# Attention block on one core: the tail's norms scaled on ScalarE, its row products and sums on GpSimd, the outputs' high half a step later

## What is computed

```python
x  = x + ga * attention(layernorm(x) * (1 + ca) + sa)      # x1 in the kernel
h  = layernorm(x) * (1 + cb) + sb                          # first norm of the tail
x  = x + gb * (layernorm(h) * ln_g + ln_b)                 # second norm of the tail
```

## Time and profile before

| | |
|---|---|
| median of 3 runs | 3386.67 us (3384.64 to 3388.11) |
| the profiled execution | 3387.18 us, span 3385.4 us |
| TensorE products busy | 3043.3 us (90%) |
| VectorE busy | 2615.7 us (77%) |
| ScalarE busy | 1756.1 us (52%) |
| GpSimd busy | 1780.8 us (53%) |
| chain that ended last | PE 43%, DVE 22%, issue 12%, POOL 6%, ACT 6% |

### The profile page before, as it was taken

How to read it: one execution, slowest core, us unless ns; L and a number is a source line. 1 busy time by engine, 2 the same in 40 slices (tenths; PEclk the granted TensorE clock), 3 DMA queues, 4 the chain that set the end, 5 groups by cost and what they waited for, 6 DMA issues and landing times.

```text
span 3385.4 us, 59145 instructions
## 1 busy us (share of the span) xinstructions
PE 3043.3 (90%) x21664; PEld 1165.7 (34%) x21664; DVE 2615.7 (77%) x4326; ACT 1756.1 (52%) x3411; POOL 1780.8 (53%) x1617
## 2 busy tenths in 40 slices
PE   3799999889989999989998999999898999999895
PEld 1323333424343332424333243433424333242221
DVE  4687777897768788797877878788786878878577
ACT  3416565655655554665545555565544555555551
POOL 2404444473536656473664736566473655736454
PEclk8769999999999999999999999999999999999997
DMA  5302020312031120312103031221313112021122
GB/s 207 101 12 63 16 69 14 95 41 71 17 95 44 43 69 31 97 45 77 45 28 111 29 92 32 62 63 29 98 32 107 32 45 80 26 76 44 40 80 69
DMA packets 180875, 205.27 MB, mean 61 GB/s; under 512 B 21460, under 2 KB 137428, under 8 KB 179428
## 3 DMA queue, kind: packets, MB, share of 16 engines
q1 hardware_dynamic: 180584, 201.50, 20.6%
HBM read 114.09 MB, written 36.50 MB: 44 GB/s over the span
## 4 chain that ended last, share of the span: by engine, by line
PE 43%; DVE 22%; issue 12%; POOL 6%; ACT 6%; DVEq 5%; POOLq 5%; DMA 2%; SPq 1%; ACTq 0%
DVE mpart L873 10%; PE ring L1113 9%; PE ps_out L1163 9%; PE ps_scores L1149 7%; PE ps_den L1180 4%; PE ps_scores L1087 4%; PE ps_den L1186 3%; PE ring L1135 3%; POOL psum L511 2%; ACT xw L661 2%; DVEq L843 2%; DVE half L850 2%; DVE dsum L889 2%; ACT xr L663 2%; POOL psum L510 2%
## 5 line engine op out<-in xcount | busy, mean ns | idle before, releaser
L713 ACT ACTIVATE prob<-ps_scores 128x512 f32<-128x512 f32 (+3 forms) x2560 | 1263.5, 536 | 1096.0 <-PE ps_scores L1152 520.7
L873 DVE TENSOR_REDUCE mpart<-ring 128x1 f32<-128x512 f32 (+3 forms) x2560 | 1401.4, 599 | 303.3 <-PE ring L1116 150.3
L1149 PE MATMUL ps_scores<-qk 98*128 98x512 f16 (+3 forms) x2560 | 880.7, 358 | 102.0 <-DVE v L855 50.0
L1113 PE MATMUL ring<-qk 96*128 96x512 f16 (+3 forms) x2560 | 882.9, 367 | 74.6 <-DVE mpart L873 64.0
L510 POOL TENSOR_TENSOR psum<-prob 128x512 f32<-128x512 f32 x360 | 483.7, 1344 | 281.9 <-ACT prob L713 161.7
L1163 PE MATMUL ps_out<-prob,v 128*32 128x512 f32 (+3 forms) x5120 | 610.9, 549 | 0.0
L1113 PEld LDWEIGHTS ring<-qk 96*128 96x128 f16 x2560 | 238.7, 99 | 895.7 <-DVE mpart L873 640.2
L496 POOL TENSOR_TENSOR xw<-xw,turn 128x512 f32<-128x512 f32 x128 | 202.2, 1580 | 582.6 <-ACT xr L663 546.7
L511 POOL TENSOR_TENSOR psum<-prob 128x512 f32<-128x512 f32 x360 | 483.2, 1342 | 0.0
L1149 PEld LDWEIGHTS ps_scores<-qk 98*128 98x128 f16 x2560 | 249.8, 100 | 419.1 <-ACT prob L713 207.3
L1087 PE MATMUL ps_scores<-hT,wg 128*128 128x512 f16 x1536 | 346.1, 382 | 3.5 <-POOL hT L501 3.5
(11 more groups left out here) (122 smaller groups left out, 2557.6 us busy)
## 6 DMA issues: line engine op xcount, KB each, us to landing
qk<-half SPq DMA_DIRECT2D x384, 128.0 KB, 3.2
turn<-in_rope_dram SPq DMA_DIRECT2D x64, 512.0 KB, 4.2
xs<-in_L_attn_x_dram SPq DMA_DIRECT2D x124, 256.0 KB, 2.8
attn_out_T<-ot SPq DMA_DIRECT2D x63, 256.0 KB, 2.1
otin<-attn_out_T SPq DMA_DIRECT2D x30, 512.0 KB, 4.7
out_dram<-x SPq DMA_DIRECT2D x60, 256.0 KB, 2.1
wg<-w_qkv_halves SPq DMA_DIRECT2D x16, 768.0 KB, 5.4
qk<-in_L_wmod_dram SPq DMA_DIRECT2D x1, 6144.0 KB, 26.7
```

Source lines behind the costliest of these rows:

```text
L713: act.activation(prob[:, s % 3, p, h % 2, 0:w], ps_scores[(HG * s + h) % NBK][:, 0:w], ACT.Exp, scale=SCALE).then_inc(exp_done, 1)
L873: dve.tensor_reduce(mpart[:, h, qt, kc:kc + 1], ring[n % NBK][:, 0:w], AX.X, ALU.max).then_inc(ring_free, 1)
L1113: mm = pe.matmul(ring[n % NBK][:, 0:w], qk[0:R, G % 2, 0, h, qt * P:(qt + 1) * P], qk[0:R, G % 2, 1, h, kc * QC:kc * QC + w], start=True, ...
L1149: mm = pe.matmul(ps_scores[k % NBK][:, 0:w], qk[0:RM, par, 1, h, kt * P:(kt + 1) * P], qk[0:RM, par, 0, h, cq * QC + q0:(cq + 1) * QC], st ...
```

## The change

The two VectorE pairs at s+4 and s+8 are gone. In their place GpSimd computes, next to 1/std, the value -mean/std (`minus_mean`: two operations of 128x1); ScalarE makes x/std - mean/std with one activation of 128x512 after the second exponential of step s+3 and of step s+7; and GpSimd multiplies by the column scale and adds the column shift, two operations of 128x512, at step s+4 (`tail_rows1`) and at s+8 (`tail_rows2`). The reciprocals' last part comes one step earlier and the high half one step later. `vector_load` no longer counts the removed pairs.

```diff
-    SLOW = {"leave": 0, 0: 1, 1: 2, 2: 3, 3: 4, "norm": 4, "high": 5, "low": 6, "store": 7}
+    SLOW = {"leave": 0, 0: 1, 1: 2, 2: 3, 3: 3, "norm": 4, "high": 6, "low": 6, "store": 7}
...
-        load += sum(c * (s - at in tail) for at, c in ((0, 1.7), (2, 2.2), (4, 4), (6, 2.2), (8, 4)))
+        load += sum(c * (s - at in tail) for at, c in ((0, 1.7), (2, 2.2), (6, 2.2)))
...
-                elif stage == 1:
-                    tail_inverse1(b, t)
-                elif stage == 3:
-                    tail_inverse2(b, t)
+                elif stage == 2:
+                    tail_shifts1(b, t)
+                elif stage == 4:
+                    tail_rows1(b, t)
+                elif stage == 6:
+                    tail_shifts2(b, t)
+                else:
+                    tail_rows2(b, t)
                 pool.drain()
...
+            def minus_mean(to, mean, inverse):
+                pool.tensor_tensor(to, mean, neg_one[:], ALU.mult)
+                pool.drain()
+                return pool.tensor_tensor(to, to, inverse, ALU.mult)
+
+            def tail_shifts1(b, t):
+                i = t % 2
+                pool.wait_ge(tail_stats1, NT * b + t + 1)
+                inv_std(rstd[:, i, :], mv[:, i, :])
+                pool.drain()
+                minus_mean(shift[:, i, :], mv[:, i, 0:1], rstd[:, i, :]).then_inc(tail_rstd1, 1)
+                pool.tensor_tensor(xs[:, i, :], x1[:, i, :], bc[:, 5, :], ALU.add)
+
+            def tail_rows1(b, t):
+                i = t % 2
+                pool.wait_ge(tail_n1, NT * b + t + 1)
+                pool.tensor_tensor(wk[:, i, :], wk[:, i, :], bc[:, 2, :], ALU.mult)
+                pool.drain()
+                pool.tensor_tensor(wk[:, i, :], wk[:, i, :], bc[:, 3, :], ALU.add).then_inc(tail_h2, 1)
...
+            def tail_rows2(b, t):
+                i = t % 2
+                pool.wait_ge(tail_n2, NT * b + t + 1)
+                pool.tensor_tensor(wk[:, i, :], wk[:, i, :], bc[:, 4, :], ALU.mult)
+                pool.drain()
+                pool.tensor_tensor(x1[:, i, :], wk[:, i, :], xs[:, i, :], ALU.add).then_inc(tail_done, 1)
...
-                        for stage in (0, 1, 3):
-                            if s - 2 * stage in tail:
+                        for stage in (0, 2, 4, 6, 8):
+                            if s - stage in tail:
...
+                            if h == 1 and s - 3 in tail_at(g, b == 0, last):
+                                tail_scaled1(b - 1, tail_at(g, b == 0, last)[s - 3])
+                            if h == 1 and s - 7 in tail_at(g, b == 0, last):
+                                tail_scaled2(b - 1, tail_at(g, b == 0, last)[s - 7])
...
+            def tail_scaled1(b, t):
+                i = t % 2
+                act.wait_ge(tail_rstd1, NT * b + t + 1)
+                act.activation(wk[:, i, :], x1[:, i, :], ACT.Identity, bias=shift[:, i, :], scale=rstd[:, i, :]).then_inc(
+                    tail_n1, 1)
...
-                elif stage == 2:
-
-                    dve.wait_ge(tail_rstd1, Z + 1)
-                    dve.scalar_tensor_tensor(wk[:, i, :], x1[:, i, :], mv[:, i, 0:1], bc[:, 2, :], ALU.subtract, ALU.mult)
-                    dve.drain()
-                    dve.scalar_tensor_tensor(wk[:, i, :], wk[:, i, :], rstd[:, i, :], bc[:, 3, :], ALU.mult, ALU.add)
-                    dve.drain()
-                elif stage == 3:
+                else:
+                    dve.wait_ge(tail_h2, Z + 1)
                     dve.bn_stats(stats[:, i, :], wk[:, i, :])
                     dve.drain()
                     dve.bn_aggr(mv2[:, i, :], stats[:, i, :]).then_inc(tail_stats2, 1)
-                else:
-                    tail_third(b, t)
```

More of the change, by code:

```diff
@@ L184, in adaln_block_kernel @@
         vare = sb("vare", [P, 2, 1], F32)
+        shift = sb("shift", [P, 2, 1], F32)
+        shift2 = sb("shift2", [P, 2, 1], F32)
         neg_half = sb("neg_half", [P, 1], F32)
+        neg_one = sb("neg_one", [P, 1], F32)
         eps_t = sb("eps_t", [P, 1], F32)
@@ L255, in adaln_block_kernel @@
                              "tail_stats2", "tail_rstd2", "tail_done"))
+        tail_n1, tail_h2, tail_n2 = (sem(n) for n in ("tail_n1", "tail_h2", "tail_n2"))
         def job_base(b):
@@ L597, in body @@
                             add_pair(G, PAIRS.index(s - 1))
-                        for stage in (0, 1, 3):
-                            if s - 2 * stage in tail:
-                                t = tail[s - 2 * stage]
+                        for stage in (0, 2, 4, 6, 8):
+                            if s - stage in tail:
+                                t = tail[s - stage]
                                 job = jobs + t // 2 + (NT // 2 if t >= 2 * T0 and not last else 0)
@@ L730, in head_high, with tail_scaled2 @@
                          x1[:, t % 2, :].rearrange("p (k q) -> p k q", k=KC)).then_inc(head_hi, 1)
+            def tail_scaled1(b, t):
+                i = t % 2
+                act.wait_ge(tail_rstd1, NT * b + t + 1)
+                act.activation(wk[:, i, :], x1[:, i, :], ACT.Identity, bias=shift[:, i, :], scale=rstd[:, i, :]).then_inc(
+                    tail_n1, 1)
+            def tail_scaled2(b, t):
+                i = t % 2
+                act.wait_ge(tail_rstd2, NT * b + t + 1)
+                act.activation(wk[:, i, :], wk[:, i, :], ACT.Identity, bias=shift2[:, i, :], scale=rstd2[:, i, :]).then_inc(
+                    tail_n2, 1)
             def leave(G, cq):
@@ L756, in head_normed @@
             def head_normed(b, t):
+                if t == 0 and b > 1:
+                    dve.wait_ge(tail_done, NT * (b - 2) + 2 * T0)
                 dve.wait_ge(head_rstd, NT * b + t + 1)
@@ L958, in tail_third @@
                 i = t % 2
+                if t == 0:
+                    dve.wait_ge(tail_done, NT * b)
                 dve.wait_ge(tail_rstd2, NT * b + t + 1)
-                dve.wait_ge(tail_x1_shift, NT * b + t + 1)
+                dve.wait_ge(tail_x1_shift, t + 1)
                 dve.scalar_tensor_tensor(wk_, wk_, mv2[:, i, 0:1], bc[:, 4, :], ALU.subtract, ALU.mult)
@@ L992, in body @@
                             n += 1
-                        for stage in range(1, 5):
-                            if s - 2 * stage in tail:
-                                tail_stage(b - 1, tail[s - 2 * stage], stage)
+                        if s - 2 in tail:
+                            tail_stage(b - 1, tail[s - 2], 1)
+                        if s - 6 in tail:
+                            tail_stage(b - 1, tail[s - 6], 2)
                         if s + 1 in head:
```

6 lines of the change are left out of this document (added).

## The result

| | before | changed |
|---|---|---|
| median, six runs each on one chip | 3387.39 us | 3449.53 us |
| range | 3381.6 to 3392.14 | 3445.86 to 3451.24 |
| profiled execution, span | 3385.4 | 3446.9 |

The change makes the kernel slower by 1.8%: ratio 1.0183, 95% interval 1.017 to 1.0197. The forecast was 3432 us, in a range of 3360 to 3490.

The account below looks back on a forecast made before the run. GpSimd, 53% busy over the span, was taken as nearly full in steps 25 to 36. Six five-tile passes at +5, three six-tile at +7 and head passes -6 made +45 us on 3387.18: 3432 us, range 3360 to 3490.

Parts of the forecast that it names:

- short waits at steps 9 and 15: Six-tile passes, where tiles are six steps apart: ScalarE's shorter waits for GpSimd, +1 us a pass.
- The dense stretch: Steps 25 to 36: GpSimd's added work makes its last pair sum late, +5.5 us with five tiles, +5 with six.
- The middle: Steps 12 to 20: row operations ahead of pair sums delay them, +2.5 us with five tiles, +2 with six.
- The wait at step 21: Six-tile passes: ScalarE's scaling waits over 5 us for GpSimd's -mean/std, holding the exponentials; +3 us a pass.
- The head passes: Three head passes: the late high half ends ScalarE's waits for GpSimd's product, -2 us each, -6 in all.
- What the change gives back: Steps 0 to 11 and 21 to 24: VectorE's relief and moved units, -3 us with five tiles, -4 with six.
- The ceiling of 79 us: Tail's passes: TensorE's extra idle time, 7.5 us with five tiles and 11.3 with six, limits any gain from rearranging the tail.
- Rival A: Tail's passes: VectorE was the limit, its relief returns two thirds of 79 us, giving 3335 us; chance 0.20.
- A scaling on ScalarE: Each 128x512 activation on ScalarE taken at 0.688 us, so 1.4 us per tile.
- GpSimd's rows operations: Each 128x512 operation at steps s+4 and s+8 takes 1.27 us, with its drain 2.85 per pair of operations.
- ScalarE's waits for pair sums: Tail's passes: these waits for GpSimd should rise from 13.4 to over 20 us a pass.
- a full block: Shared port: VectorE's two-input and GpSimd's operations block each other wholly; doubted, as 1.73 us is less than 1.27 + 0.74.

Follow-up runs that it names:

- Experiment 4: Changed kernel with half of GpSimd's row operations left out (first norm's column shift, second norm's column scale): 3377.31 us, 0.9977 of the kernel before.
- Experiment 6: Changed kernel with both ScalarE scalings behind the fourth exponential of their step instead of the second: 3443.05 us, 1.0165 of the kernel before.
- experiment 2: Kernel before with only the changed kernel's outputs' table (reciprocals' last part one step earlier, high half one later): 3407.89 us, ratio 1.0066.
- experiment 3: Kernel before with only the high half one step later, reciprocals as before: 3385.69 us, ratio 1.0001.
- Experiment 7: Kernel before without VectorE's four 128x512 operations per tile, the change's planner loads, old table, tail's result not computed: 3290.09 us, ratio 0.9715.
- experiment 12: Changed kernel with only the first norm moved, the second left on VectorE, and the old outputs' table: 3360.02 us, 0.9929 of the kernel before.
- experiment 9: Changed kernel with only the first norm moved, the second left on VectorE, new table: 3384.29 us, 0.9991 of the kernel before.
- experiment 10: Changed kernel with only the second norm moved, the first left on VectorE, new table: 3441.72 us, 1.016 of the kernel before.
- experiment 8: Kernel before with VectorE's four operations per tile replaced by one-input statistics operations, planner and table as before, tail's result not computed: 3326.93 us, ratio 0.983.
- experiment 5: Changed kernel with all row operations on VectorE, scalings still on ScalarE, planner's loads as before, new table: 3447.11 us, 1.0183 of the kernel before.

## Why the prediction was right, and which terms were not

The direction, the place and the main cause came as forecast. That the total is only 17 us off is partly luck, since larger errors cancel in it. The terms of the sum by the stretches in which the prediction put them, in us a pass (its 1 us for short waits at steps 9 and 15 is in the third line, as is step 21):

| steps | five tiles: forecast | measured | six tiles: forecast | measured |
|---|---|---|---|---|
| 25 to 36 | +5.5 | +6.1 | +5 | +3.1 |
| 12 to 20 | +2.5 | +4.4 | +2 | +3.7 |
| 0 to 11 and 21 to 24 | -3 | -4.4 | -4 +3 +1 = 0 | -1.7 |
| 37 to the next pass | 0 | 0.0 | 0 | -0.9 |
| sum | +5 | +6.2 | +7 | +4.2 |

**The dense stretch: right for five tiles.** +5.5 us, measured 5.9 to 6.5 in the six passes; the chain on GpSimd grew by 7.5 against 7.0. Six tiles: +5, measured 1.9, 4.7 and 2.8. Experiment 4 shows that it is GpSimd's load.

**The middle: right in sign, too small.** In steps 12 to 20 the passes grew by 4.4 and 3.7 us. In experiment 4, with half of the row operations gone, 0.9 and nothing are left of it, so here too it is GpSimd's load. The wait at step 21 was forecast at more than 5 us and measured 2.67 to 2.96. Experiment 6 shows that such waits are hardly a cost beside GpSimd's lateness but the place where it shows: adding 3 and 1 us for them counted it twice.

**The head passes: wrong sign.** I took -2 us each for waits of ScalarE that end; they came out +3.2, +4.8 and +2.8. The step that failed is reading the table as a matter of ScalarE's waits alone. Experiments 2 and 3 place the cost in the two reciprocals in one step of VectorE and the units that the planner then gives to the next, and show that ending those waits is worth nothing. This term, 16.8 us off, is by itself the difference between +45 and the measured +62; the five-tile passes' 6.9 more and the six-tile passes' 8.4 less nearly cancel. In the tail's passes I put the table at nothing; experiment 2 shows 8 us in the five-tile passes, and experiment 12 against 9 shows 21.

**What the change gives back: too small.** Experiment 7 measured 96 us for VectorE's relief. Not all of that stands against the 30 us of the prediction's last term, which covered steps 0 to 11 and 21 to 24 only: there experiment 7 gives 39. The prediction took more off GpSimd's chain, for the lengthening that ends: 2.8 us in the dense stretch with five tiles, which is what experiment 7 measures, 3.6 with six, where it measures 8.1, and 1.8 in the middle with six, where it measures 2.9. Together that makes some 63 us of relief in the prediction against the 96. The ceiling of 79 us on any gain was wrong too: it counted only the idle time of TensorE beyond that of a pass without tail, but its busy time fell as well, from 3043.3 to 3001.8 us, though single products lasted as long as before (the value products of 128x512, L1163, 617 and 618 ns). Rival A was right that the relief is large and wrong on the sum.

Since the total came out near the forecast, what is put in its place must have been undervalued as well: 62 + 96 - 8 to 21 for the table leaves some 137 to 150 us for GpSimd's row operations, the -mean/std and the scalings. This is a difference of measured runs and holds as far as their effects add up, which experiments 9, 10 and 12 show to be rough. Half of the row operations carry 72 of it (experiment 4). In the dense stretch with five tiles both sides, what GpSimd takes on and what the end of the lengthening gives back, were priced in GpSimd's own chain, and there the forecast was within 0.6 us.

**Smaller terms.** A scaling on ScalarE takes 0.82 us, not 0.69. GpSimd's rows operations take 1.27, as taken. GpSimd's busy time rose by 214 us, not 280 to 340, for the most part since its pair sums lost 51 us. VectorE's fell by 193, not 220. ScalarE's waits for pair sums did not rise above 20 us a pass but fell to 8.8; they stand at the scalings now, 29.8 together. GpSimd is busy 92%, not over 95%, of the dense stretch: the gaps of some 0.15 us behind drains do not count as busy.

**Open.** Why the second norm is so much dearer to move than the first. The pair that stays on VectorE is 0.7 us per tile longer then; by the 59 us for 1.8 us in experiment 8 that could be some 23 of the 57 us (an estimate), and no run tests it. The planner's loads, and with them the units of the steps, differ between the two as well. The second norm's two row operations come at s+8, where a later tile's statistics or sum stand in the same step, and moving them by a step gave 8 of 57 us. Its scaling at s+7 waits for -mean/std behind the next tile's sum. How much each of these counts, no run separates. Nor is it known why the table costs more in the tail's passes when the first norm alone is moved than with none or both, or how the 39 us of experiment 5 divide between ScalarE's time, the waits and GpSimd's small operations.

## What to carry to other kernels

An engine that is busy 53% over the span can be nearly full in the twelve steps that matter: price what is moved to it in its own chain there, operation by operation with the drains. Price the relief by a run that leaves the work out, with the planner's loads held fixed, and not by the idle time of the engine that waits, and move the parts one at a time: here half of the move, with the outputs' table left alone, gained 0.7% where the whole lost 1.8%. Ending a wait of ScalarE was worth nothing where what it waited for was late anyway; look for the same microseconds at the next wait.

## What the runs showed of the hardware

VectorE's operations with two SBUF inputs and GpSimd's additions lengthen each other (1.61 for 0.74, 1.73 for 1.27). This is a matter of tens of microseconds here: with statistics operations of one SBUF input in their place, GpSimd's pair sums took 1.27 us on average instead of 1.34, and 59 us came back.

The prediction held against a full block that 1.73 is less than 1.27 + 0.74. The rows do not speak against one. The two operations in front of those of the earlier trace rows, in the kernel before:

```profile
1306.05 1.27 POOL L511 TENSOR_TENSOR psum<-prob 128x512 f32<-128x512 f32 x1
1306.33 1.54 DVE L915 SCALAR_TENSOR_TENSOR wk<-x,mv,bc 128x512 f32<-128x512 f32 x1
```

The ends are 1307.32 (GpSimd), 1307.87 (VectorE), 1309.01 (GpSimd) and 1309.55 (VectorE). Each operation begins inside the other engine's and ends 0.54 to 1.14 us behind its end. That fits engines that take turns, where each waits only for what is left of the other's operation. It does not prove it: with 1.27 and 0.74 us counted from the other's end, the last three would end 0.13 to 0.20 us later than they do.

TensorE's granted clock was not the same in all windows of stalled steps. In steps 25 to 36 of a six-tile pass it was 1.00 before, 0.94 in the changed kernel and 0.89 in experiment 5; TensorE was idle 6.8, 8.1 and 10.2 us in them. A mean below 1.00 is a part of the window at 1.2 GHz instead of 2.4. In the changed kernel TensorE was busy 6.36 of the 10.30 us from 2575.0 to 2585.3, at a clock of 1.00, and in the 3.5 us behind that the clock was 0.51. Its busy time in the stretch rose from 46.99 to 50.37 us for about the same number of products, so some of what the stalls cost in those passes was paid in slower products.
